# A new order for all five engines, small-tile work gathered, program blocks pinned, fixed PSUM banks and a fourth group slot in a four-layer cross-attention kernel

## The chip, the cores and the metric

The kernel runs on one core of one Trainium2 chip. The metric is the device time of that core in microseconds, the median of several executions; lower is better. TensorE (PE in the profile) multiplies, VectorE (DVE) and ScalarE (ACT) do elementwise work and empty PSUM, GpSimd (POOL) does elementwise work in SBUF, and SyncE (SP) issues DMAs.

## What is computed

Four cross-attention layers run one after the other on `x` (128 sequences of 64 tokens, 128 channels). Every layer attends to the same context `ctx_2048` (128 sequences of 64 tokens, 256 channels). All is float32. Layer 0 has 16 heads of 64 channels, a bias on a few key columns, and a dense output projection with bias:

```python
q = hidden_states @ Wq;  k = encoder @ Wk;  v = encoder @ Wv        # 16 heads of 64
logits = einsum('bhqd,bhkd->bhqk', q, k) * 64**-0.5 + col_bias      # 64 x 64 per head
out = einsum('bhqk,bhkd->bhqd', softmax(logits), v)
x = out @ Wo + bo + x
```

Layers 1 to 3 normalise `x` first (rmsnorm with a weight), have 16 query heads of 8 channels on 4 key and value heads, and add their output to `x`:

```python
q = (rmsnorm(x, norm_w) @ wq)      # (T, 4 kv heads, 4 repeats, 8)
k = cond @ wk;  v = cond @ wv      # (S, 4, 8)
attn = softmax(einsum('btgrd,bsgd->bgrts', q, k) / 8**0.5)
x = x + einsum('bgrts,bsgd->btgrd', attn, v) @ wo
```

## The kernel before, in words

The batch is cut into 32 groups (`NG`) of 4 sequences, 256 tokens a group; `x` and the context lie transposed, channels on partitions. A group's work is a set of steps, each named (kind, group, layer, part). A step's TensorE part, and what empties it, are:

- `k`, `v`, `k3`, `q0` (L935 to L969): projections of context and x for layer 0, and the small keys of layers 1 to 3 (`k3`); 128x128 weights, moving 256 to 374 columns. ScalarE copies them out.
- `s` of layer 0 (L980): scores, in 64x64 tiles of the array; VectorE adds the bias (`add`), takes the maximum (`max`), GpSimd subtracts (`sub`), ScalarE takes `exp`, VectorE `sum` and `rcp`, GpSimd normalises (`nrm`).
- `s` of layers 1 to 3 (L991): scores in 32x64 tiles; VectorE `max` and `sub`, ScalarE `exp` with the rmsnorm factor `inv` as its scale, VectorE `sum` and `rcp`, GpSimd `nrm`.
- `t` (L1009): transposes of the normalised scores, 64 rows by 128 columns each, with an identity as the moving operand; ScalarE copies them back (`et`).
- `pv0` (L1019, 64x64 tiles), `pv` of layers 1 to 3 (L1055, 128x32 tiles): probabilities times values. `wo0` (L1027) and `wo` (L1063): output projections in the full array, added to x by VectorE.
- `x2` (L1038): x transposed with full 128x128 identities, squared by ScalarE, summed by VectorE (`ssq`), turned into `inv` on GpSimd (`ms`). `q` (L1032): the query projection of layers 1 to 3.

Every fp32 matmul of the source is two matmul instructions in the trace, a transpose is one. Matmuls with fewer rows or columns than 128 use a part of the array, so that two to sixteen of them can run side by side.

SyncE loads x (`lt`) and context (`cT`) for three groups on, stores a group's result (`st`), and for layers 1 to 3 spreads the small keys into block-diagonal tiles (`kr`, 16 DMAs a layer and group, 48 a group, L858). All of it goes through one queue in a written order.

The order on each engine comes from tables of slots, one per engine (`PE_TIME`, `ACT_TIME`, and so on): a step of group g stands at g x `PERIOD` + its slot, and `timed` sorts the steps by that. Tables with the suffix `_ENDS` replace the slots of the groups at both ends (0 to 2 and 28 to 31). The slots set an order only; at run time each engine takes its list in order and waits on counting semaphores. A period of TensorE's list holds steps of four groups: projections of one, layer 0 of the next, layers 1 to 3 of older ones. The last two groups (`SPLIT`) are worked in halves of 128 tokens.

Three slots (`NS`) hold the per-group tiles `xT`, `QT`, `E`, `stat`, `inv`, `nt`; a group reuses those of the group three before it. The eight PSUM banks are given out while the program is written: a step takes the banks that, by the slot tables (`DUE`), come free first (`bank_of`), and waits for whoever emptied them last (`before`, `emptied`). An `s` step of layers 1 to 3 takes two adjacent pairs. A `t` step takes four banks, two for each half, and waits for each half by itself, inside one step.

Of the kernel before, what the change touches and what calls it, by code (L numbers as in the profile page):

```python
# [18 lines left out]
NS = 3  # L19
# [11 lines left out]

# [3 lines left out]

PERIOD = 42.042923
PE_TIME = {
    "k": {0: (-412.51237, -392.85979, -393.50182, -378.96658)},
    "v": {0: (-362.26897, -361.57101, -345.3867, -356.85139, -354.42587, -354.15549)},
    "k3": {0: (-370.81423,)},
    "q0": {0: (-376.11391, -371.17844, -371.03544, -374.58041)},
    "s": {0: (-370.42581, -370.43581), 1: (-331.1163,), 2: (-294.56971,), 3: (-270.23591,)},
    "t": {0: (-348.90236,), 1: (-317.45557,), 2: (-285.56016,), 3: (-253.49293,)},
    "pv0": {0: (-336.97107, -339.47402)},
    "wo0": {0: (-335.52959,)},  # L50
    "x2": {1: (-333.51029,), 2: (-300.02901,), 3: (-272.27314,)},
    "q": {1: (-333.36356,), 2: (-297.92571,), 3: (-272.42144,)},
    "pv": {1: (-307.00785,), 2: (-275.6979,), 3: (-251.97787,)},
    "wo": {1: (-306.84954,), 2: (-274.17148,), 3: (-249.78271,)},
}
ACT_TIME = {
    "k": {0: (-159.40091, -139.84623, -139.98107, -130.14834)},
    "v": {0: (-113.28983, -107.6489, -91.26426, -99.3201, -101.51439, -100.50468)},
    "k3": {0: (-118.80598,)},
    "q0": {0: (-126.45335, -120.46805, -119.7705, -121.20179)},  # L60
    "exp": {0: (-104.71249, -107.45298, -104.13778, -112.0564),
            1: (-72.87501, -75.24855, -75.86332, -77.67646),
            2: (-46.48173, -42.853, -38.45332, -45.85794),
            3: (-13.61974, -15.46628, -16.07173, -9.25001)},
    "et": {0: (-94.43216, -92.88175, -94.18051, -93.30054),
           1: (-65.47568, -65.49475, -67.04523, -58.9258),
           2: (-29.57269, -30.6792, -29.39678, -29.30645),
           3: (-5.91218, -5.28672, -5.87163, -4.79848)},
    "pv0": {0: (-88.61505, -90.21177)},
    "x2": {1: (-80.71806,), 2: (-48.9703,), 3: (-20.92127,)},  # L70
    "q": {1: (-83.14394,), 2: (-49.01262,), 3: (-21.83589,)},
    "pv": {1: (-54.62611,), 2: (-28.54234,), 3: (-2.96356,)},
}
DVE_TIME = {
    "add": {0: (-111.81915, -113.85763, -116.32868, -114.4835)},
    "max": {0: (-111.12099, -111.9694, -109.50874, -113.03448),
            1: (-78.27865, -78.64191, -80.16737, -81.16307),
            2: (-49.4951, -47.30671, -44.89232, -48.09597),
            3: (-18.00057, -19.96031, -20.47661, -12.65384)},
    "sum": {0: (-105.85858, -108.79654, -105.82451, -108.85157),  # L80
            1: (-74.06889, -72.89305, -74.39011, -76.6622),
            2: (-45.82444, -42.12155, -39.90611, -43.17731),
            3: (-11.25879, -13.61973, -15.19198, -8.91803)},
    "rcp": {0: (-105.30454, -105.8339, -104.88475, -105.95459),
            1: (-73.24416, -72.5981, -74.25837, -75.30566),
            2: (-43.71754, -41.14225, -36.69635, -42.40837),
            3: (-8.99609, -11.86286, -13.00823, -8.45231)},
    "wo0": {0: (-85.86089,)},
    "ssq": {1: (-83.37942,), 2: (-50.06193,), 3: (-24.55834,)},
    "sub": {1: (-75.05879, -76.58249, -77.57201, -79.06871),  # L90
            2: (-47.48804, -44.41007, -42.7565, -47.06613),
            3: (-15.77249, -17.39509, -18.78085, -11.73353)},
    "wo": {1: (-52.80331,), 2: (-24.91929,), 3: (0.43953,)},
}
POOL_TIME = {
    "sub": {0: (-109.0751, -112.84247, -103.46541, -114.27942)},
    "nrm": {0: (-96.88446, -97.18383, -96.68759, -99.16105),
            1: (-77.33025, -74.7097, -77.44776, -81.07111),
            2: (-47.81451, -39.53916, -39.48291, -39.86483),
            3: (-10.89236, -10.98157, -11.60033, -9.93748)},  # L100
    "ms": {1: (-90.05711,), 2: (-48.08021,), 3: (-16.64786,)},
}
SP_TIME = {
    "cT": {0: (-79.98433,)},
    "kr": {1: (-146.01496,), 2: (-158.22011,), 3: (-95.52327,)},
    "lt": {0: (-85.21396,)},
    "st": {0: (-22.10277,)},
# [15 lines left out]
    },
    1: {
        "k": {0: (-566.91726, -566.84726, -566.85909, -495.94114)},
        "v": {0: (-429.86277, -454.09358, -429.42785, -432.53711, -410.26388, -409.41835)},
        "k3": {0: (-451.20253,)},
        "q0": {0: (-443.81064, -543.11196, -443.80064, -566.90726)},
        "s": {0: (-435.74448, -435.73448), 1: (-361.36903,), 2: (-293.48868,), 3: (-270.59363,)},
        "t": {0: (-398.16561,), 1: (-327.25449,), 2: (-283.08701,), 3: (-254.95664,)},  # L130
        "pv0": {0: (-391.3161, -392.15936)},
        "wo0": {0: (-369.64937,)},
        "x2": {1: (-363.56604,), 2: (-294.08881,), 3: (-271.1829,)},
        "q": {1: (-365.31926,), 2: (-294.87445,), 3: (-272.68924,)},
        "pv": {1: (-319.44014,), 2: (-276.55088,), 3: (-252.35751,)},
        "wo": {1: (-303.22232,), 2: (-272.96424,), 3: (-250.92766,)},
    },
    2: {
        "k": {0: (-477.83204, -474.8597, -452.75348, -474.26973)},
        "v": {0: (-397.59961, -370.32494, -366.3626, -399.37273, -393.74967, -369.82342)},  # L140
        "k3": {0: (-436.78293,)},
        "q0": {0: (-438.05897, -412.93857, -411.14663, -405.14797)},
        "s": {0: (-401.02958, -370.42598), 1: (-332.3726,), 2: (-294.80438,), 3: (-270.32365,)},
        "t": {0: (-345.90875,), 1: (-316.53142,), 2: (-285.32115,), 3: (-252.84676,)},
        "pv0": {0: (-335.7855, -336.0694)},
        "wo0": {0: (-335.19552,)},
        "x2": {1: (-333.7359,), 2: (-307.00405,), 3: (-272.73062,)},
        "q": {1: (-332.77139,), 2: (-306.92719,), 3: (-272.48453,)},
        "pv": {1: (-312.76983,), 2: (-277.23482,), 3: (-251.66785,)},
        "wo": {1: (-310.567,), 2: (-275.19735,), 3: (-250.15637,)},  # L150
    },
    28: {
        "k": {0: (-412.71099, -395.62776, -394.66559, -374.46511)},
        "v": {0: (-372.72927, -370.61535, -348.22122, -356.11236, -372.30535, -369.1062)},
        "k3": {0: (-372.90485,)},
        "q0": {0: (-376.19535, -376.52669, -372.80769, -378.85152)},
        "s": {0: (-366.08291, -370.42578), 1: (-333.69106,), 2: (-294.56964,), 3: (-290.9334,)},
        "t": {0: (-348.95635,), 1: (-316.43043,), 2: (-291.45239,), 3: (-289.21552,)},
        "pv0": {0: (-337.34252, -348.14089)},
        "wo0": {0: (-335.38944,)},  # L160
        "x2": {1: (-335.13648,), 2: (-305.96072,), 3: (-291.1191,)},
        "q": {1: (-335.12648,), 2: (-295.55608,), 3: (-291.1291,)},
        "pv": {1: (-312.12718,), 2: (-291.32735,), 3: (-288.30154,)},
        "wo": {1: (-311.7751,), 2: (-291.19727,), 3: (-287.41173,)},
    },
    29: {
        "k": {0: (-416.8347, -394.81034, -399.13617, -389.50576)},
        "v": {0: (-375.72257, -375.58124, -353.93453, -354.84901, -372.30905, -368.8995)},
        "k3": {0: (-379.11161,)},
        "q0": {0: (-392.62609, -376.79767, -375.64799, -377.27179)},  # L170
# [432 lines left out]
        "st": {0: (-73.11023, -81.94464)},  # L603
    },
}
SPLIT = range(NG - 2, NG)
LATE = range(NG - 2, NG)


# [713 lines left out]
```

## Time and profile before

| | us |
|---|---|
| runs of the kernel before | 1378.57, 1382.42, 1383.25 |
| median | 1382.42 |
| span of the profiled execution | 1376.3 |
| own time of the profiled execution outside that span | not given by the page |
| TensorE busy in it | 1362.7 |
| VectorE, ScalarE, GpSimd busy | 1064.6, 1003.3, 734.9 |

The span runs from the first to the last instruction of the core; a run's time has what lies around it as well. A share of busy time is an average over the span. For matmuls the profile models the end, and those that run side by side overlap, so TensorE's share says that it always has something under way, not that it is at its peak; the distance from one step's start to the next one's is what a step takes. Line numbers are those of the kernel before.

### The profile page before, as it was taken

The page shows a single profiled execution, that of the slowest core. Times are in us where ns is not written, and L with a number is a line of the kernel's source. Part 1 is how long each engine was busy: PE and PEld are TensorE (multiplying, and loading weights), DVE is VectorE, ACT ScalarE, POOL GpSimd, SP SyncE. Part 2 cuts the span into 40 slices and gives each one's busy share as a digit, 9 for nine tenths or more (in the row PEclk, how much of TensorE's full clock was granted, in tenths as well). Part 3 has the DMA queues.
Part 4 walks back from the last instruction along what each step waited for, and adds up shares of the span by engine and source line. Part 5 has one row for each costly group of instructions (what it writes and reads, how often), then busy time and mean ns, then how long its engine had stood idle before and what let it go on. Part 6 is the DMA issues. An engine that isn't in the chain of part 4 may idle for free.

```text
span 1376.3 us, 59054 instructions
## 1 busy us (share of the span) xinstructions
PE 1362.7 (99%) x25494; PEld 1055.6 (77%) x25494; DVE 1064.6 (77%) x2258; ACT 1003.3 (73%) x2207; POOL 734.9 (53%) x851
## 2 busy tenths in 40 slices
PE   9999999999999999999999999999999999999997
PEld 7777777777777777777787777777777777777875
DVE  4487777987778977778777788777798777778776
ACT  4667777767778677777677786777776777767886
POOL 5355456654456545466554565544665445655553
PEclk9999999999999999999999999999999999999999
DMA  5010010000000010100001001001011010010000
GB/s 151 18 30 22 15 34 16 26 27 23 26 23 22 27 27 23 28 18 26 26 24 26 23 22 27 27 24 28 17 27 27 23 27 25 19 36 22 7 23 14
DMA packets 46003, 37.02 MB, mean 27 GB/s; under 512 B 17072, under 2 KB 41520, under 8 KB 45744
## 3 DMA queue, kind: packets, MB, share of 16 engines
q1 hardware_dynamic: 44576, 32.89, 8.8%
q8 instruction: 201, 3.29, 1.0%
q14 instruction: 58, 0.48, 0.1%
q10 hardware_dynamic: 1168, 0.36, 0.1%
HBM read 16.42 MB, written 4.19 MB: 15 GB/s over the span
## 4 chain that ended last, share of the span: by engine, by line
PE 95%; ACT 2%; DVE 2%; issue 0%; POOL 0%; DMA 0%; SPq 0%; POOLq 0%
PE psum L954 18%; PE psum L942 16%; PE psum L1009 10%; PE psum L1027 8%; PE psum L969 8%; PE psum L991 7%; PE psum L1055 7%; PE psum L1019 5%; PE psum L980 5%; PE psum L1063 4%; PE psum L1032 3%; PE psum L961 2%; PE psum L1038 2%; ACT E L1141 1%; ACT E L1136 1%; DVE st L1226 1%
## 5 line engine op out<-in xcount | busy, mean ns | idle before, releaser
L892 POOL TENSOR_TENSOR E<-E,st 128x512 f32<-128x512 f32 x488 | 497.3, 1044 | 168.1 <-DVE st L1238 159.4
L1136 ACT ACTIVATE E<-E,inv 128x512 f32<-128x512 f32 x384 | 273.4, 722 | 135.8 <-DVE E L1230 134.3
L1226 DVE TENSOR_REDUCE st<-psum 128x8 f32<-128x512 f32 x372 | 240.4, 673 | 145.5 <-PE psum L991 145.1
L1235 DVE TENSOR_REDUCE st<-E 128x8 f32<-128x512 f32 x488 | 321.2, 665 | 35.3 <-ACT E L1129 28.2
L1141 ACT COPY E<-psum 128x512 f32<-128x512 f32 x512 | 275.1, 609 | 33.7 <-PE psum L1009 33.5
L954 PE MATMUL psum<-wv,cT 128*128 128x374 f32 (+1 forms) x768 | 273.3, 486 | 0.3 <-issue 0.3
L1230 DVE TENSOR_TENSOR E<-psum,st 128x512 f32<-128x512 f32 x372 | 248.3, 677 | 0.3
L904 POOL TENSOR_TENSOR nt<-nt,powers 128x2 f32<-128x2 f32 (+1 forms) x102 | 19.9, 196 | 420.0 <-DVE nt L1265 400.2
L942 PE MATMUL psum<-cT,wk 128*128 128x256 f32 x1024 | 240.5, 383 | 0.2 <-DMA cT<-in_ctx_t 0.2
L942 PEld LDWEIGHTS psum<-cT,wk 128*128 128x128 f32 x1024 | 191.5, 190 | 34.8 <-issue 1.5
L954 PEld LDWEIGHTS psum<-wv,cT 128*128 128x128 f32 x768 | 138.2, 189 | 73.5 <-ACT V L1097 8.5
L888 POOL TENSOR_TENSOR E<-E,st 128x512 f32<-128x512 f32 x140 | 142.6, 1044 | 35.8 <-DVE st L1220 13.1
L1009 PE MATMUL psum<-ident,E 64*128 64x64 f32 x4096 | 156.6, 226 | 3.5 <-issue 1.4
L1009 PEld LDWEIGHTS psum<-ident,E 64*128 64x128 f32 x4096 | 138.3, 139 | 20.0 <-issue 8.0
L969 PE MATMUL psum<-xq,wq 128*128 128x256 f32 x512 | 129.0, 385 | 0.0
L1027 PE MATMUL psum<-QT,wo 128*128 128x256 f32 (+1 forms) x544 | 119.1, 372 | 0.5 <-ACT QT L1163 0.5
L1055 PEld LDWEIGHTS psum<-E,VB 128*32 128x32 f32 x6144 | 90.9, 110 | 37.1 <-issue 14.7
L1097 ACT COPY V<-psum 128x374 f32<-128x374 f32 (+1 forms) x192 | 87.3, 456 | 42.9 <-PE psum L954 42.1
L1121 ACT ACTIVATE QT<-psum 128x512 f32<-128x512 f32 x128 | 75.9, 599 | 56.5 <-PE psum L969 48.2
L969 PEld LDWEIGHTS psum<-xq,wq 128*128 128x128 f32 x512 | 94.8, 190 | 23.1 <-issue 10.8
L991 PE MATMUL psum<-KB,QT 32*64 32x256 f32 x3072 | 109.2, 388 | 1.6 <-ACT QT L1160 1.0
L1027 PEld LDWEIGHTS psum<-QT,wo 128*128 128x128 f32 x544 | 96.2, 190 | 14.8 <-ACT QT L1163 0.6
(68 smaller groups left out, 1632.2 us busy)
## 6 DMA issues: line engine op xcount, KB each, us to landing
KB<-K SPq DMA_DIRECT2D x1536, 8.0 KB
cT<-in_ctx_t SPq DMA_DIRECT2D x32, 256.0 KB, 2.8
xq<-in_x_t SPq DMA_DIRECT2D x32, 128.0 KB, 2.1
out<-xT SPq DMA_DIRECT2D x30, 128.0 KB, 1.8
wk<-in_L_xattn_Wk SPq DMA_DIRECT2D x3, 256.0 KB, 5.8
wv<-in_L_xattn_Wv SPq DMA_DIRECT2D x2, 374.0 KB, 8.6
wq<-in_L_xattn_Wq SPq DMA_DIRECT2D x1, 512.0 KB, 7.7
wo<-in_L_xattn_Wo SPq DMA_DIRECT2D x1, 512.0 KB, 4.4
```

The source lines that it names most:

```text
L892: e.tensor_tensor(E3, E3, wide(stat[s][u][:, 16:24]), ALU.mult).then_inc(g_nrm.sem, 1)
L942: m = e.matmul(bank[:, T * jj:T * jj + T], wk0[:, k, 128 * j:128 * j + 128], cTg[:, k, :], start=(k == 0), stop=(k == 1))
L954: m = e.matmul(bank[:, 0:hi - lo], cTg[:, k, 128 * p:128 * p + 128], wv[:, k, lo:hi], start=(k == 0), stop=(k == 1))
L969: m = e.matmul(bank[:, T * jj:T * jj + T], wq0[:, 128 * j:128 * j + 128], xq[g % NX][:, :], start=True, stop=True)
L991: m = e.matmul(psum[64 * b2:64 * b2 + 64, at[r], 256 * p:256 * p + 256], QT[s][lo:lo + 32, 0, 64 * b:64 * b + 64], KB[l - 1][g % 2][lo:lo ...
L1009: m = e.transpose(psum[:, at[2 * n + i], c:c + 64], E[s][2 * p + r][rows, 128 * k:128 * k + 128], ident[rows, rows])
L1027: m = e.matmul(bank[:, tokens], wo0[:, j, :], QT[s][:, j, tokens], start=(j == 0), stop=(j == 7))
L1136: e.activation(E[s][u][:, :], E[s][u][:, :], ACT.Exp, scale=inv[s][:, u // 2:u // 2 + 1]).then_inc(a_exp.sem, 1)
L1141: e.copy(E[s][u][:, :], psum[:, i, :]).then_inc(a_et.sem, 1)
L1226: e.tensor_reduce(stat[s][u][:, 0:8].rearrange("p (r h) -> p r h", r=2), scores_of[g, l, u], AX, ALU.max).then_inc(d_max.sem, 1)
L1230: e.tensor_tensor(pairs(E[s][u][:, :]), scores_of[g, l, u], stat[s][u][:, 0:8].rearrange("p (r h a) -> p r h a", r=2, a=1).to_broadcast([1 ...
L1235: e.tensor_reduce(stat[s][u][:, 8:16], heads(E[s][u][:, :]), AX, ALU.add).then_inc(d_sum.sem, 1)
```

## The change

1. All slot tables are new. `PERIOD` is 41.111607 instead of 42.042923 (both only scale the ordering). Groups 0 to 6 and 26 to 31 have tables of their own, and those replace a group's slots altogether. The new order gathers the steps that use small tiles. From one `wo0` to the next TensorE's list was (kind and layer; brackets around small-tile steps; letters without a layer are layer 0 or projections):

```
before: wo0 q0 wo3 x2.1 q1 q0 [s1] q0 q0 k3 k [s0 s0 t2] v v [pv2 t1] wo2 v q3 x2.3 v [s3] v k k [pv1 t0] wo1 v
        x2.2 q2 [pv0 t3 pv0] k [s2 pv3]
after:  wo0 q0 q1 q0 [s1 x2.1 t3.1] k q0 v v k3 [t3.0 t2.1 s0 s0 t1.1 t1.0 t2.0] k k [pv3 pv2 pv1] wo3 wo2 q0 q3
        [x2.3 t0.0 t0.1 s3] v k wo1 v v q2 [pv0 s2 x2.2 pv0] v
```

Over all groups the list changes between full-array and small-tile steps 470 times before and 384 times after.

2. A `t` step is one half of a group (`t` part 0 and part 1), with its own slot, two banks and its own waits; it was both halves in one step.
3. `x2` is done as transposes of 64 rows, the same tile shape as `t`: four instead of two per group and layer, into two adjacent banks. ScalarE's square reads both banks with a strided pattern.
4. Before the steps in `FRESH` (part 1 of `t` in layers 0 and 3; other sets at the ends) the TensorE program is aligned to a multiple of 256 instructions. The loader branches over the padding.
5. The banks of each step stand in tables (`PE_BANKS`, `BANK_ENDS`); `DUE` and the search are gone.
6. `NS` is 4 instead of 3.

```diff
-NS = 3
+NS = 4
...
-PERIOD = 42.042923
+PERIOD = 41.111607
 PE_TIME = {
...
-    "t": {0: (-348.90236,), 1: (-317.45557,), 2: (-285.56016,), 3: (-253.49293,)},
+    "t": {0: (50.12134, 50.61734), 1: (81.13632, 80.58731), 2: (122.74371, 119.08386), 3: (159.64587, 152.83728)},
...
+FRESH = {("t", 0, 1), ("t", 3, 1)}
+FRESH_ENDS = {
+    0: {("t", 0, 1), ("t", 3, 1)},
+    1: {("t", 3, 1)},
+    2: {("t", 3, 1)},
+    3: {("t", 0, 1), ("t", 3, 1)},
+    4: {("t", 0, 1), ("t", 3, 1)},
+    5: {("t", 0, 1), ("t", 3, 1)},
+    6: {("t", 0, 1), ("t", 3, 1)},
+    26: set(),
+    27: {("pv0", 0, 1), ("q0", 0, 2), ("v", 0, 4), ("wo", 3, 0), ("x2", 3, 0)},
+    28: set(),
+    29: {("t", 1, 0)},
+    30: {("pv0", 0, 0), ("v", 0, 3), ("x2", 3, 1)},
+    31: set(),
+}
...
-        for kind, layers in {**table, **{k: {**table.get(k, {}), **v} for k, v in at_ends.get(g, {}).items()}}.items():
+        for kind, layers in at_ends.get(g, table).items():
...
-DUE = {tuple(st): at for at, *st in ACT_TIMED + DVE_TIMED}
+
+
+def banks_of(kind, g, l, u):
+
+    return [int(i) for i in BANK_ENDS.get(g, PE_BANKS)[kind][l][u]]
...
-            return [[st]] * (2 if kind == "pv0" else 1)
+            return [[st]] * (2 if kind in ("pv0", "x2") else 1)
...
-            evictors = held_until(st)
-            if st[0] == "s" and l > 0:
-                at = min(([i, i + 1, j, j + 1] for i in range(5) for j in range(i + 2, 7)),
-                         key=lambda four: max(free[i] for i in four))
-            else:
-                at = sorted(sorted(range(8), key=lambda i: free[i])[:len(evictors)])
+            evictors, at = held_until(st), banks_of(*st)
+            assert len(at) == len(set(at)) == len(evictors)
...
-                if kind != "t":
-                    emptied(w, [ev for evs in before[st] for ev in evs])
+                emptied(w, [ev for evs in before[st] for ev in evs])
+                if (kind, l, u) in FRESH_ENDS.get(g, FRESH):
+                    e.addr_align(256, max_nops=0)
...
                     for p in halves(g, u):
-                        m = e.transpose(bank[:, 128 * p:128 * p + 128], xT[s][:, 128 * p:128 * p + 128], ident[:, :])
+                        for i in range(2):
+                            rows = slice(64 * i, 64 * i + 64)
+                            m = e.transpose(psum[:, at[i], 64 * p:64 * p + 64], xT[s][rows, 128 * p:128 * p + 128],
+                                            ident[rows, rows])
...
+                    p = halves(g, u)
+                    x = psum[:, at[0]:at[0] + 2, 64 * p[0]:64 * p[-1] + 64].rearrange("t i (p c) -> t i p c", c=64)
+                    sq = QT[s][:, 2, tokens].rearrange("t (p i c) -> t i p c", i=2, c=64)
...
-                        e.activation(QT[s][:, 2, tokens], bank[:, tokens], ACT.Square).then_inc(a_ev.sem, 1)
+                        e.activation(sq, x, ACT.Square).then_inc(a_ev.sem, 1)
```

## Rows read from the trace of the kernel before

**Rows 1.** The page, part 1: busy us, share of the span, instructions.

```profile
PE 1362.7 (99%) x25494; PEld 1055.6 (77%) x25494; DVE 1064.6 (77%) x2258; ACT 1003.3 (73%) x2207; POOL 734.9 (53%) x851
```

**Rows 2.** The page, part 4: shares of the chain by engine.

```profile
PE 95%; ACT 2%; DVE 2%; issue 0%; POOL 0%; DMA 0%; SPq 0%; POOLq 0%
```

**Rows 3.** Windows: stretch, its length, busy us of each engine (instructions), clock.

```profile
160.00:1120.00 960.00, 957.42 (x17869) 742.01 (x17868) 763.64 (x1626) 713.56 (x1559) 526.86 (x598) 1.00 0.09 24
...
1330.00:1376.00 46.00, 38.23 (x1084) 28.41 (x1082) 32.89 (x62) 31.51 (x74) 16.01 (x26) 1.00 0.06 17
```

**Rows 4.** TensorE timeline, steady: start, us, line, tile, count.

```profile
681.67 1.42 PE L954 MATMUL psum<-wv,cT 128*128 128x374 f32 x4
682.93 0.59 PE L1032 MATMUL psum<-xT,wqs 128*128 128x256 f32 x2
...
683.58 1.42 PE L954 MATMUL psum<-wv,cT 128*128 128x374 f32 x4
684.93 1.12 PE L991 MATMUL psum<-KB,QT 32*64 32x256 f32 x32
685.98 1.52 PE L954 MATMUL psum<-wv,cT 128*128 128x372 f32 x4
687.33 3.62 PE L942 MATMUL psum<-cT,wk 128*128 128x256 f32 x16
...
694.84 0.38 PE L1038 MATMUL psum<-ident,xT 128*128 128x128 f32 x2
695.05 0.60 PE L1032 MATMUL psum<-xT,wqs 128*128 128x256 f32 x2
...
696.67 1.21 PE L1009 MATMUL psum<-ident,E 64*128 64x64 f32 x32
697.82 1.16 PE L1019 MATMUL psum<-E,V 64*64 64x64 f32 x64
...
701.88 1.10 PE L1055 MATMUL psum<-E,VB 128*32 128x64 f32 x64
702.91 3.72 PE L1027 MATMUL psum<-QT,wo 128*128 128x256 f32 x16
```

**Rows 5.** TensorE timeline near the end: t in a half, pv in four runs.

```profile
1340.36 0.71 PE L1009 MATMUL psum<-ident,E 64*128 64x64 f32 x16 [0.22 <-ACT E L1136]
1341.00 0.49 PE L1063 MATMUL psum<-QT,wos 128*128 128x128 f32 x2
...
1357.97 0.65 PE L1049 MATMUL psum<-E,ones 128*32 128x64 f32 x32
...
1359.89 1.07 PE L1063 MATMUL psum<-QT,wos 128*128 128x128 f32 x4
```

**Rows 6.** Timeline: first wo0 matmuls of groups 3, 17 and 26.

```profile
156.08 1.78 PE L1027 MATMUL psum<-QT,wo 128*128 128x256 f32 x7
...
744.76 1.56 PE L1027 MATMUL psum<-QT,wo 128*128 128x256 f32 x6
...
1123.28 1.99 PE L1027 MATMUL psum<-QT,wo 128*128 128x256 f32 x8
```

**Rows 7.** Timeline: a t step stopped in its middle.

```profile
632.05 0.90 PE L1009 MATMUL psum<-ident,E 64*128 64x64 f32 x22
633.94 0.53 PE L1009 MATMUL psum<-ident,E 64*128 64x64 f32 x10 [0.99 <-issue]
```

**Rows 8.** The page, part 3: the queue that brings instructions.

```profile
q8 instruction: 201, 3.29, 1.0%
```

**Rows 9.** SyncE timeline: copies of the small keys.

```profile
672.09 10.99 SPq L858 DMA_DIRECT2D KB<-K  x16
...
683.62 21.67 SPq L858 DMA_DIRECT2D KB<-K  x32
```

**Rows 10.** Timeline: group 0, s1 and its t.

```profile
44.40 1.12 PE L991 MATMUL psum<-KB,QT 32*64 32x256 f32 x32
...
65.43 1.21 PE L1009 MATMUL psum<-ident,E 64*128 64x64 f32 x32
```

More of the change, by code:

```diff
@@ L65 @@
[L65 to L72, printed above, removed]
+    "k": {0: (2.50397, 14.44440, 4.26196, -8.93698)},
@@ L73 @@
+    "pv0": {0: (62.41330, 60.00031)},
+    "x2": {1: (70.81265,), 2: (102.44397,), 3: (132.58655,)},
+    "q": {1: (68.69162,), 2: (100.48978,), 3: (132.33356,)},
+    "pv": {1: (88.79163,), 2: (129.00702,), 3: (169.71564,)},
 }
 DVE_TIME = {
[L75 to L79, printed above, removed]
@@ L88 @@
[L88 to L93, printed above, removed]
+    "add": {0: (38.62964, 39.22464, 39.81964, 40.41464)},
+    "max": {0: (41.60565, 42.20166, 41.00964, 42.79767),
+            1: (72.65164, 73.84564, 71.13165, 70.53564),
+            2: (103.35898, 102.76297, 104.87897, 102.16696),
+            3: (136.96619, 135.17413, 137.56219, 134.57812)},
@@ L138 @@
-    2: {
[L139 to L150, printed above, removed]
+        "k": {0: (29.85090, 26.29356, 28.12423, 32.41656)},
@@ L173 @@
[L173 to L178 removed]
+        "k": {0: (-11.60978, -11.61170, -11.61362, -63.42667)},
+        "v": {0: (52.38427, 61.31826, 42.08233, -11.60956, 46.31366, 3.65048)},
@@ L481 @@
+        "sum": {0: (63.13143, 61.71542, 52.88674, 57.06078)},
+        "rcp": {0: (64.54147, 64.43246, 58.85079, 62.90743)},
+        "wo0": {0: (76.73003, 73.08739)},
+        "sub": {1: (89.49072, None, 87.58172, None),
[5 rows of a table added]
     },
     31: {
[L483 to L487 removed]
@@ L502 @@
+        "wo0": {0: (55.97612, 60.60253)},
+        "sub": {1: (65.93248, None, 70.23485, None),
[5 rows of a table added]
     },
@@ L603 @@
-        "st": {0: (-73.11023, -81.94464)},
-    },
+        "cT": {0: (12.16878,)},
+        "kr": {1: (38.07344,), 2: (49.82106,), 3: (72.22179,)},
+        "lt": {0: (83.27184,)},
+        "st": {0: (107.63390, 108.70116)},
+    },
+}
+PE_BANKS = {
+    "k": {0: ("6", "7", "0", "6")},
+    "v": {0: ("5", "4", "2", "7", "0", "5")},
+    "k3": {0: ("1",)},
+    "q0": {0: ("6", "6", "7", "4")},
+    "s": {0: ("17", "63"), 1: ("0123",), 2: ("1245",), 3: ("0123",)},
+    "t": {0: ("54", "67"), 1: ("01", "42"), 2: ("57", "25"), 3: ("40", "47")},
+    "pv0": {0: ("03", "30")},
+    "wo0": {0: ("0",)},
+    "x2": {1: ("56",), 2: ("67",), 3: ("01",)},
+    "q": {1: ("7",), 2: ("1",), 3: ("7",)},
+    "pv": {1: ("3",), 2: ("2",), 3: ("5",)},
+    "wo": {1: ("6",), 2: ("2",), 3: ("4",)},
+}
@@ L759, in xattn_kernel @@
             for i, evs in zip(at, evictors):
-                held[i], free[i] = evs, max(DUE[ev] for ev in evs)
+                held[i] = evs
             if st[0] == "s" and l == 0:
```

1395 lines of the change are left out of this document (977 added, 418 removed), and 102 rows, old and new, of tables (BANK_ENDS, DVE_ENDS, PE_ENDS).

## The prediction

> **What bounds the kernel now.** I read the busy shares first, then the windows, then the chain, then TensorE's order of work in time. TensorE is busy 1362.7 us of a span of 1376.3 [rows 1]; VectorE has 77%, ScalarE 73%. The chain that ended last is TensorE for 95% [rows 2]. Between 160 and 1120 us TensorE is busy 957.42 of 960 us at full granted clock, while VectorE has 763.64, ScalarE 713.56 and GpSimd 526.86; only in the last 46 us does TensorE idle much, 46.00 - 38.23 = 7.8 us [rows 3]. So nothing that waits elsewhere is worth anything between the ends. What is left is the time that TensorE spends on what it does, and that depends on order: in the steady stretch each step has a fixed time set by its neighbours, to 0.01 us [rows 4]. The reader is to look there at start-to-start times, not at the second column, in which a matmul's end is modelled and overlaps the next.
>
> **Price of a change of tile shape.** The same v step of 4 matmuls takes 681.67 to 682.93 = 1.26 us between full-array steps, 683.58 to 684.93 = 1.35 before a 32x64-tile step, and 685.98 to 687.33 = 1.35 behind one (372 columns there, so 1.25 undisturbed) [rows 4]. A full-array run between small-tile steps thus pays 0.09 + 0.10 = 0.19, which I round to 0.20. The small side pays too. A t step with 32 transposes takes 697.82 - 696.67 = 1.15 us, one with 16 takes 1341.00 - 1340.36 = 0.64 [rows 4, 5]; 16 more cost 0.51, so the run itself holds 0.64 - 0.51 = 0.13, say 0.14 (other t rows give 1.14). Sixty-four pv matmuls take 702.91 - 701.88 = 1.03; 128 in one run, four rows of x32, take 1359.89 - 1357.97 = 1.92; the second 64 cost 0.89, and a run holds 0.14 [rows 4, 5]. A row of neighbours of the same shape pays each price once.
>
> The Trainium skill says why, in TensorEngine Tiling (Array Packing), Key Properties: a change of tiling mode drains the engine, a change of tile within a mode does not. It gives no price. The trace has one, but it shows more than the sentence: a small-to-small change costs as well.
>
> **The change, part by part.**
> (1) The order of TensorE. I counted runs of one shape over the two lists of steps, from one wo0 to the next. Before: full 7, s 3, 64x64 tiles (s0 and pv0) 3, t 4, pv 3. After, in five small stretches of the steady period (six is the mean with the ends, 384 / 2 / 32): full 5, s 3, 64x64 3, t with x2 5, pv 1. The difference is 2 x 0.20 full + 2 x 0.14 pv - 1 x 0.14 t = 0.54 us a group.
> (2) x2 becomes four 64-row transposes into two banks. Now it is 0.21 us in a full run [rows 4], three times a group; at t's rate, 0.51 / 16 = 0.032 each, four cost 0.13. Gain 3 x 0.085 = 0.26. The runs that it breaks are in (1). The bounds are 0.63 (x2 vanishes beside its neighbours) and -0.16 (each x2 pays 0.14 more than I counted). I take 0.26, from the t rows, whose tile shape and operands it has.
> Together 0.80 us a group. Undisturbed, a period takes 744.76 - 702.91 = 41.85 us [rows 4, 6]; it becomes 41.05. There are 23 such periods, 156.08 to 1123.28, so 18.4 us. At the ends the groups have orders of their own. Over all, full/small changes drop from 470 to 384, that is 43 stretches fewer, of which the 23 periods give 46; same-shape runs drop from 659 to 620, 39 fewer against 69 in the steady part (20 to 17 a period). So the ends have 30 runs more, at 0.14 some 4.3 us, less 9 groups x 0.26 = 2.3 for x2: 2.0. Work: -18.4 + 2.0 = -16.4.
> (3) Alignment. The mean of the 23 periods is 967.20 / 23 = 42.05, 0.20 more than an undisturbed one, 4.6 us in all [rows 6]. The rows of a stall show what it is: a t step stops in its middle for 0.99 us with no one to blame but "issue" [rows 7]. The instruction queue brought 201 packets of 3.29 MB / 201 = 16.4 KB [rows 8]; TensorE has 2 x 25494 = 50988 loads and matmuls, 254 a packet. So the program comes in blocks of 256 instructions, 128 matmuls, and a block that is used up in 2 us outruns the next one. The five stalls of the steady part all stand in small-tile runs, this one behind 128 s0 matmuls. After, the dense places are denser: three pv in a row are 192 matmuls in 3 x 0.89 + 0.14 = 2.8 us. The two alignments pin where blocks begin: from t0.1 to t3.1 are 302 matmuls, 2.4 blocks, from there to the next t0.1 486, 3.8. Walking the order with the times above, the shortest block (rest of s0, three t, a little k) lasts 3.8 us, the one that holds most of the pv run 4.7. I take all 4.6 us as gone (bounds 0, and +1 us a group, below). By a page's rule it would be otherwise: the Trainium skill, Runtime: NRT & Kernel Launch, Instruction fetch mechanics, holds the crossing of a block boundary for mostly hidden. Then nothing is gained here and the time is that of rival E; rows 7 speak against it.
> What alignment adds is a jump over the padding, 59 in all (38 in groups 7 to 25, 12 before, 9 after) and one block more to fetch in most groups. No row shows a jump on TensorE. From below it is 0: the target block was asked for a whole block ago, and instructions already queued cover it. From above it is a full stall, 0.99 us each [rows 7]. I take 0, the nearest case being the clean boundaries, six a group, that leave periods at 41.85.
> (4) Four slots. From q0 to the last wo a group now stays in flight for 4.0 periods; slots only keep that legal. SP's queue: the 48 KB copies a group take 10.99 + 21.67 = 32.7 us of the period [rows 9]; with the loads and the store 34.1 of 41.05. From k3 to s1 of the same group TensorE has 34 us of other steps, and two sets of copies and their landing need about 24, so 10 us cover this. An added wait there would hold the x load and the context load queued behind it, each needed two periods later.
> (5) Banks. Fixed ones change no duration. x2 now needs two; VectorE's and ScalarE's part is unchanged, and their shares become 763.64 / 957.42 x 41.85 / 41.05 = 81% and 76%, nowhere a bound. What is queued behind a t that waits for its bank is all of TensorE, so an error there costs in full (second rival).
> (6) The ends. In flight for a period more, the first group runs with less beside it. Before, s1 of group 0 starts at 44.40 and its t at 65.43, 21 us later [rows 10]; in the new order only eight steps, x2, q0, k, two v, k3 and two s0, about 9 us, stand between, and VectorE alone needs four units of max, sub, sum and reciprocal, 4 x 1.9 = 7.6, plus an exp and a normalisation of 1.0, 9.5 to 10. That is a wait of about 1 us, and I count six such places in groups 0 to 2. At the far end the last 46 us hold 7.8 us of idle already [rows 3], and the new list interleaves groups 28 to 31 more finely. Bounds 0 and 12 us more idle; I take 8, as much again as the end has now.
>
> **Sum.** -16.4 - 4.6 + 8 = -13.0 us on a span of 1376.3, so 1363.3. The profiled span lies 6.1 under the median of the runs, 1382.42 (runs 1378.57 to 1383.25); the page gives no other time of its own execution. I keep the 6.1: 1369.4 us, 0.9% faster.
>
> **Rivals.**
> (A) No extra idle at the ends, gain in full: 1369.4 - 8 = 1361. For it, the start of before loses only little; against, the short chain of (6). 0.10.
> (B) TensorE waits once a group, on a bank or a normalisation, because steps of one shape now stand together and their evictions come in bursts: ten copies of transposes of 0.5 us each around one stretch, with 3.5 us of k before the pv. A wait of 0.5 us in 23 groups gives back 11.5: 1381. For it, bursts; against, 19 to 24% spare time on both engines and nothing in rows 3 that waits. 0.13, half of it ending below 1378.
> (C) A jump over padding stalls TensorE. Each costs up to 0.99 us [rows 7]; the change turns slower from 13.0 / 59 = 0.22 us a jump; at 0.5 us it is +29.5, 1399. For it, jumps stand inside small-tile stretches, where the queue is drained fastest; against, clean boundaries cost nothing. 0.08. The Trainium skill, Runtime: NRT & Kernel Launch, Instruction fetch mechanics, speaks of a stall when a taken branch leaves the two pages held; the target here is the next page, so by it this rival is out.
> (D) The dense runs outrun the fetch in spite of the alignment, because a block of 3.8 us is still too short: about 1 us a group, +23, 1392. 0.05. One block of 2 us stalled in before, one of 3.8 did not show, so the threshold lies between.
> (E) The small stalls stay as they are, 0.20 us a period, because jumps and the more frequent fetches give back what pinned boundaries save: 1369.4 + 4.6 = 1374. For it, one fetch more in most groups; against, the densest blocks are the ones pinned away. 0.08.
>
> **Chances and range.** The forecast has 0.56, with 1363 to 1374 as its own range (extra idle 2 to 12). What a measurement of this kernel tells from no change is about 0.3%, 4.1 us. Faster: 0.56 + 0.10 + 0.08 and half of B, 0.06, = 0.80; same: the rest of B and 0.01 of mild C = 0.08; slower: C and D, 0.12. The range goes from 1360 to 1386: it leaves out the strong forms of C and D.
>
> **What would show it.** wo0 to wo0 at 41.0 to 41.1 us in nearly every steady period, with no long "issue" gap; one pv run of x192 of about 2.8 us; x2 at 0.13 beside t; the v steps beside small tiles still at 1.35. A period of 41.3 to 41.6 with releasers named is B; gaps before t0.1 and t3.1 are C; gaps in the middle of pv or s0 are D. TensorE idle in the first 130 and the last 60 us should be about 18 us, where it is 10 now. If undisturbed periods come out at 41.85, the price of a shape change was misread and the prediction is wrong at its root.

## The result, and the profile after

| | before | after |
|---|---|---|
| time, median of the runs | 1381.6 us (1378.57 to 1383.25) | 1430.9 us (1420.92 to 1433.51) |
| profiled execution: time, span | -, 1376.3 us | 1430.16, 1428.4 us |

The ratio is 1.034, 95% interval 1.031 to 1.038. I had predicted 1369.4 us, 0.9% faster; it became 3.4% slower, outside the range.

The page after, part 1, then the instruction queue of part 3 and the chain's shares of part 4:

```profile
PE 1370.1 (96%) x25686; PEld 1058.6 (74%) x25686; DVE 1081.4 (76%) x2258; ACT 1018.0 (71%) x2207; POOL 734.2 (51%) x851
...
q8 instruction: 223, 3.65, 1.1%
...
PE 80%; DVE 10%; POOL 5%; issue 2%; ACT 2%; DVEq 0%; POOLq 0%
```

TensorE was 99% busy [rows 1] and is 96%: 58 us of the span idle where there were 14. It works only 7 us longer. There are 22 block fetches more [rows 8]. TensorE's share of the chain fell from 95% [rows 2] to 80%, as it seems because the chain runs through releasers that are falsely named for the long waits below; in d2, a run below that has none of these waits, it is 93%. The windows say where, and the list of TensorE's waits of after (total us, times, longest) says at which tile:

```profile
160.00:1120.00 960.00, 924.61 (x17340) 718.53 (x17339) 750.11 (x1564) 695.22 (x1501) 503.71 (x572) 0.99 0.09 24
1382.40:1428.40 46.00, 37.84 (x1170) 28.90 (x1154) 34.00 (x67) 33.48 (x73) 17.98 (x28) 1.00 0.06 18
```

```profile
PE psum L1602 <- POOL E L1486: 29.8, 19, 2.7
PE psum L1602 <- issue: 6.2, 23, 0.7
```

The steady stretch idles 35.4 us (2.6 before, [rows 3]), the last 46 us little more than before (8.2 against 7.8). L1602 is the t step. The view names GpSimd's normalisation as the releaser of 19 waits. Four of them, 1.6 us, stand in the first 110 us. The other 15, 28.2 us, stand in the steady stretch; there the normalisation had been done, as the runs below show, and "issue" would be the right word. A long wait ahead of t3.1, one with the half clock behind it, and the same place without a stall (timeline of after):

```profile
611.58 0.34 PE L1633 MATMUL psum<-ident,xT 64*128 64x64 f32 x4
614.13 0.71 PE L1602 MATMUL psum<-ident,E 64*128 64x64 f32 x16 [2.21 <-POOL E L1486]
...
655.69 0.34 PE L1633 MATMUL psum<-ident,xT 64*128 64x64 f32 x4
658.09 1.12 PE L1602 MATMUL psum<-ident,E 64*128 64x64 f32 x16 [2.05 <-POOL E L1486]
659.13 3.08 PE L1537 MATMUL psum<-cT,wk 128*128 128x256 f32 x8
662.05 1.03 PE L1564 MATMUL psum<-xq,wq 128*128 128x256 f32 x4
...
701.14 0.34 PE L1633 MATMUL psum<-ident,xT 64*128 64x64 f32 x4
701.31 0.66 PE L1602 MATMUL psum<-ident,E 64*128 64x64 f32 x16
701.95 1.99 PE L1537 MATMUL psum<-cT,wk 128*128 128x256 f32 x8
703.78 1.03 PE L1564 MATMUL psum<-xq,wq 128*128 128x256 f32 x4
```

x2 to t takes 2.55, 2.40 and 0.17 us. The record of the jump itself, the branch over the padding (L1523), tells the first of these places from the last: it took 2782 ns where the t came late and 297 ns where it did not (views of L1523 around either):

```profile
L1523 PEldq COMPARE_BRANCH  x1: 2782/2782/2782, 611.3 to 611.3; - x1
...
L1523 PEldq COMPARE_BRANCH  x1: 297/297/297, 700.9 to 700.9; - x1
```

Of the 23 jumps ahead of t3.1 in groups 3 to 25, 16 stall so: x2 to t takes 1.0 to 3.1 us, 0.8 to 2.9 over the 0.17. Behind 658.09 the same eight k matmuls take 662.05 - 659.13 = 2.92 us instead of 1.83, and the t ahead of them 1.04 instead of 0.64: the granted clock was 0.5 for 3.4 us, as at three other places, each behind one of these stalls (x2 to t 2.0 to 2.4 us). Behind the five longest stalls, 2.55 to 3.07 us, it stayed at 1.0. The other jump, between t0.0 and t0.1, has its gap in every group, and the dense run of pv is as predicted, 719.55 - 716.73 = 2.82 us, with no stall in it:

```profile
694.25 2.11 PE L1620 MATMUL psum<-QT,wo 128*128 128x256 f32 x9
...
716.73 2.89 PE L1651 MATMUL psum<-E,VB 128*32 128x64 f32 x192
719.55 1.13 PE L1659 MATMUL psum<-QT,wos 128*128 128x256 f32 x4
...
722.08 0.66 PE L1602 MATMUL psum<-ident,E 64*128 64x64 f32 x16
722.99 0.71 PE L1602 MATMUL psum<-ident,E 64*128 64x64 f32 x16 [0.26 <-issue]
...
736.14 2.12 PE L1620 MATMUL psum<-QT,wo 128*128 128x256 f32 x9
```

t to t takes 0.91 us here and 0.5 without a jump; over the whole period the jump costs 0.47 (41.89 here, 41.42 in d1 below, whose other steps are the same). And the period without a long stall, 736.14 - 694.25 = 41.89 us, is no shorter than before (41.85, [rows 4, 6]).

### The profile page after: what moved, and what is told of

It reads as the page before. It is cut to its first block, busy times and chain, and to the rows that moved or that the text cites. A ratio compares the mean times of both kernels' runs of the same rounds, so it can differ in the third digit from the quotient of the medians.

```text
span 1428.4 us, 59381 instructions
## 1 busy us (share of the span) xinstructions
PE 1370.1 (96%) x25686; PEld 1058.6 (74%) x25686; DVE 1081.4 (76%) x2258; ACT 1018.0 (71%) x2207; POOL 734.2 (51%) x851
## 4 chain that ended last, share of the span: by engine, by line
PE 80%; DVE 10%; POOL 5%; issue 2%; ACT 2%; DVEq 0%; POOLq 0%
PE psum L1537 16%; PE psum L1549 15%; PE psum L1602 10%; PE psum L1586 6%; PE psum L1651 6%; PE psum L1564 5%; POOL E L1486 5%; PE psum L1575 4%; PE psum L1620 4%; PE psum L1612 4%; PE psum L1659 3%; DVE E L1828 3%; DVE st L1824 3%; PE psum L1625 3%; DVE st L1833 2%
## 5 line engine op out<-in xcount | busy, mean ns | idle before, releaser
L1737 ACT COPY E<-psum 128x512 f32<-128x512 f32 x512 | 266.6, 599 | 76.3 <-PE psum L1602 73.2
L1732 ACT ACTIVATE E<-E,inv 128x512 f32<-128x512 f32 x384 | 260.2, 720 | 40.1 <-POOL inv L1500 29.3
L1537 PE MATMUL psum<-cT,wk 128*128 128x256 f32 x1024 | 249.8, 392 | 1.0 <-ACT KT L1685 0.7
L1828 DVE TENSOR_TENSOR E<-psum,st 128x512 f32<-128x512 f32 x372 | 243.8, 683 | 0.4
L1602 PE MATMUL psum<-ident,E 64*128 64x64 f32 x4096 | 163.3, 226 | 41.2 <-POOL E L1486 29.8
L1602 PEld LDWEIGHTS psum<-ident,E 64*128 64x128 f32 x4096 | 141.9, 139 | 69.5 <-POOL E L1486 32.3
L1685 ACT COPY KT<-psum 128x512 f32<-128x512 f32 x128 | 75.8, 592 | 49.6 <-PE psum L1537 48.9
L1811 DVE TENSOR_TENSOR E<-psum,bias 128x512 f32<-128x512 f32 x128 | 80.4, 684 | 24.2 <-PE psum L1575 24.1
```

Source lines behind the costliest of these rows:

```text
L1537: m = e.matmul(bank[:, T * jj:T * jj + T], wk0[:, k, 128 * j:128 * j + 128], cTg[:, k, :], start=(k == 0), stop=(k == 1))
L1602: m = e.transpose(psum[:, at[i], c:c + 64], E[s][2 * u + r][rows, 128 * k:128 * k + 128], ident[rows, rows])
L1732: e.activation(E[s][u][:, :], E[s][u][:, :], ACT.Exp, scale=inv[s][:, u // 2:u // 2 + 1]).then_inc(a_exp.sem, 1)
L1737: e.copy(E[s][u][:, :], psum[:, i, :]).then_inc(a_et.sem, 1)
L1828: e.tensor_tensor(pairs(E[s][u][:, :]), scores_of[g, l, u], stat[s][u][:, 0:8].rearrange("p (r h a) -> p r h a", r=2, a=1).to_broadcast([1 ...
```

## The experiments

"Mean period" is from group 3's wo0 to group 25's, in 22 parts: 42.03 us before, 43.67 after.

**a1, a2, a3, b1: where the stalls come from.** a1 is after with all alignments taken out; a2 lacks only those at t3.1, a3 only those at t0.1; b1 is before with two added.

```
a1  -  if (kind, l, u) in FRESH_ENDS.get(g, FRESH): e.addr_align(256, max_nops=0)
a2  +  if (kind, l, u) in FRESH_ENDS.get(g, FRESH) - {("t", 3, 1)}: ...
a3  +  if (kind, l, u) in FRESH_ENDS.get(g, FRESH) - {("t", 0, 1)}: ...
b1  +  if 2 < g < 26 and (kind, l, u) in {("t", 0, 0), ("t", 3, 0)}: e.addr_align(256, max_nops=0)
```

> The changed kernel without any alignment of the program; all else as changed. Theory J (the jumps over padding stall TensorE, because the block jumped to is fetched late): the gaps of up to 2.5 us before part 1 of t in layer 3 and of 0.3 us before part 1 of t in layer 0 go; undisturbed periods come to 41.0 to 41.4 us, small stalls stay where a block is used up inside pv or s0; time 1365 to 1385. Rival O (the new order itself waits, on GpSimd's normalisation as the profile names it): the gaps stay, time 1420 to 1440. Rival F (without pinned blocks the dense pv run outruns the fetch in many groups): gaps of about 1 us in pv or s0 in most groups, time 1390 to 1410.

> The changed kernel with the alignment before part 1 of t in layer 3 taken out and all others kept. Theory J: the 2 us gaps go, the 0.3 us ones at layer 0 stay, plus a random stall where block ends fall badly: 1375 to 1395. Rival O: 1420 to 1440.

> The changed kernel with only the alignment before part 1 of t in layer 0 taken out. If the 2 us gap depends on the block that is jumped from being left early (50 matmuls in), its size changes with the new place of the block ends: a group has now 1.6 thousand instructions between two jumps and leaves its last block after about 60 instructions. Theory J: still some gap before part 1 of t in layer 3, 0 to 3 us a group, time 1380 to 1440. Rival O: 1420 to 1440 with gaps as they were.

> The kernel before, order and banks untouched, with the same alignment before t of layer 0 and t of layer 3 in groups 3 to 25. Theory J: each of the 46 jumps costs 0.3 to 2.5 us by where it leaves its block, so 1395 to 1450 against 1382, with gaps only before these t steps. Rival O: the alignment is harmless, 1375 to 1385.

Measured: a1 1417.8 us (ratio 1.027, 1.025 to 1.029), a2 1506.8 (1.091, 1.088 to 1.095), a3 1463.7 (1.062, 1.056 to 1.068), b1 1434.4 (1.038, 1.036 to 1.041); mean periods 42.76, 46.88, 45.26 and 44.25. Only b1 fell where I had expected it. a1 came out between the ranges of its theories, and a2 and a3 above all of theirs, so the first form of the theory was too mild: one badly placed jump a group costs more than two. In b1 nothing but two jumps a group came into the old order, and it has after's stall and its false releaser (waits of b1):

```profile
PE psum L1011 <- POOL E L892: 35.5, 20, 3.2
```

So the alignment is guilty: b1 has the order and the normalisation of before. But without alignment the new order is slow as well. Its waits in a1 (L1649 pv, L1600 t, L1573 s0):

```profile
PE psum L1649 <- issue: 13.2, 12, 1.6
PE psum L1600 <- issue: 5.0, 10, 1.1
PE psum L1573 <- issue: 4.2, 5, 1.2
```

That is rival D's mechanism: dense runs outrun the fetch. All but one of its "issue" gaps in the steady stretch end 2.3 to 3.0 us after a fetch began. a2 and a3 show what makes a jump dear. I walked the order with its undisturbed times: in a2 52 instructions stand in the last block ahead of the jump, used up in 1.8 us, and another block lasts 2.1 us; in a3 the last one is used up in 1.1 us. The block behind the jump seems to be asked for only when the last block is entered, and from the fetch's start to the next matmul the traces show 2.3 to 3.1 us, median 2.5 (116 stalled jumps of after, a2, a3, b1, c1, c2, e1 and f2).

**c1, c2, f2: where the boundaries fall.** Only the slots of the two alignments differ from after (here a slot is the place in a block of 256 at which the aligned step begins).

```
c1  e.addr_align(256, offset=16 if l == 0 else 0, max_nops=0)
c2  e.addr_align(256, offset=16 if l == 0 else 32, max_nops=0)
f2  e.addr_align(256, offset=8 if l == 0 else 0, max_nops=0)
```

> The kernel after, with t0.1 aligned to slot 16 of a block instead of slot 0, so that every block boundary up to t3.1 comes 16 instructions earlier; the last of them then lies inside wo0 and no longer just ahead of q's wait for wo0's eviction. Theory J (a jump is free only if the block behind it was asked for some 3 us or more before, and TensorE's sequencer cannot ask while it stands at a wait close behind the boundary): the stalls ahead of t3.1, 0.9 to 3.0 us in 16 of 22 periods, vanish in all of them, the half-clock stretches of 3.4 us that followed them too, the 0.475 us a group at t0.1 stay. Mean period 43.67 -> 41.9 to 42.0, time 1430 - 38 = 1392 (1386 to 1400). Rival P (each jump over padding has a price of its own, whatever block it leaves): nothing changes by more than 0.1 us a group, 1428 to 1432. Rival O (the t3.1 steps wait for GpSimd's normalisation): the same 1428 to 1432.

> As c1, and t3.1 aligned to slot 32, so that the boundaries behind it come 32 instructions earlier. In the walk through the undisturbed times of the order, one block then holds s0, three t and no k and is used up in 2.6 us (in c1 the shortest takes 3.8). Theory J, with blocks coming at least some 3.5 us apart: a stall of about 0.9 us inside s0 or t in nearly every group, mean period 42.8, time c1 + 20 = 1412 (1402 to 1420), although the number of jumps and fetches is that of c1. Rival P: as c1 within 3 us.

> The kernel after with t0.1 at slot 8, t3.1 at slot 0: the last boundary lies 20 instructions ahead of q's wait (12 in after: 16 of 22 groups stalled; 27 in c1: none). Theory H: stalls of 1 to 3 us ahead of t3.1 in some 5 to 12 of 22 groups, mean period 42.4 to 43.2, time 1408 to 1427. Rival L (it is the length of the last block that decides, 103 instructions here, 95 in after, 111 in c1, with a sharp limit): every group the same, either 1402 or 1430, and the fetch ahead of the jump always starts at the same distance from the boundary.

Measured: c1 1401.8 us (1.014, 1.012 to 1.016), c2 1413.2 (1.022, 1.020 to 1.024), f2 1429.1 (1.037, 1.033 to 1.041). Sixteen slots took 29 us away. In c1 none of the t3.1 jumps stalls and nearly every period is 41.9, though nothing of the normalisation was changed; the waits at t keep only the small gap of t0.1:

```profile
PE psum L1602 <- issue: 5.7, 23, 0.3
```

c1's time was 10 us over my figure: the mean period, 42.08, was only 0.1 over; 8.0 us lie behind group 25, and most of them at one place. There the jump ahead of an aligned x2 stalls in c1 (a branch of 3.93 us) and not in after (0.39), and a half-clock stretch of 6.8 us follows it. The steps from the q in front of it to the second q0 behind take 16.07 us instead of 10.22. The x2 in c1:

```profile
1262.67 0.48 PE L1633 MATMUL psum<-ident,xT 64*128 64x64 f32 x4 [3.35 <-issue]
```

The same jump stalls in e1, f1 and f2 (2.8 to 3.4 us), so the times of these runs hold it as well; mean periods do not. c2 lost 0.55 us a group to its 2.6 us block, where I had said 0.9. f2 corrects the theory: with 20 instructions between the boundary and q's wait 17 of 23 jumps stall, about as with 12, and I had expected 5 to 12 of them. The start of the last fetch relative to the jump has two values in after and f2: 5.2 to 7.3 us ahead (no stall), or between 1.4 us ahead and 0.8 behind; in c1 only the first. The wait itself dates them. q waits for wo0's addition to x, and passes 4.3 us after wo0 begins. In groups 3 to 24 of after, f2, c1 and of e1 and f1 below, the last fetch starts 2.5 to 4.6 us ahead of that moment in all 67 jumps without a stall, and 0.9 to 3.1 us behind it in all 43 with one, never between. So the request is held by the wait or it is not. With 23 instructions (e1) 10 of 22 jumps stall, with 27 (c1) and 31 (f1) none, so the limit lies between 23 and 27 instructions. Why the same code comes out one way in one group and the other way in the next is open. The Trainium skill, Runtime: NRT & Kernel Launch, Instruction fetch mechanics, says that the sequencer fetches the next page while it executes the current one. The traces agree, with one fetch for every 256 instructions [rows 8] and the early fetches above, and add that the fetch can be held back by a wait in the current one.

**c3, d3, d1, c4: the price of a jump itself.** One alignment a group, in full-array steps with long blocks around it.

```
c3  after emptied(...):   if 2 < g < 26 and (kind, l, u) == ("v", 0, 4): e.addr_align(256, offset=64, max_nops=0)
d3  the same lines, ahead of emptied(...)
d1  if 2 < g < 27 and (kind, l, u) == ("q0", 0, 3): e.addr_align(256, offset=160, max_nops=0)
c4  before.py: if 3 < g < 27 and (kind, l, u) == ("q0", 0, 0): e.addr_align(256, offset=32, max_nops=0)
```

> The kernel after with one alignment a group (3 to 25) instead of two, at v4, a full-array step, to slot 64. In the walk no block of the group is used up in less than 4.0 us, and the block left by the jump lasts 5.8 us. Theory J: the jump costs about 0.1 us, the stalls inside pv, t and s0 go. Mean period 41.5 (41.40 undisturbed, 42.76 without alignment, 43.67 with the two); time 1417.8 - 28 = 1390 (1385 to 1396), the rest over the kernel before being its ends. Rival F (the dense run of 192 pv matmuls outruns the fetch wherever blocks begin): stalls of 1 to 1.8 us in pv stay in many groups, 1405 to 1418. Rival P: 0.5 us or more for each of 23 jumps, 1400 or more.

> The kernel before with one alignment a group (4 to 26), at the first q0 behind wo0, to slot 32. In the walk no block is used up in less than 3.8 us. Theory J: the 4.6 us of small fetch stalls go, 23 jumps at 0.1 us come: 1380.3 - 4.6 + 2.3 = 1378 (1375 to 1381), period 41.95 in every group. Rival P: 23 x 0.5 = 11 us or more on top, 1388 or more (two alignments at t0.0 and t3.0 gave 1434).

> The kernel with one alignment a group at v4 and slot 64, with the alignment put ahead of v4's wait for its bank instead of behind it; nothing else differs. In that kernel the trace has the wait, then a branch of 0.30 to 0.38 us, then the matmul, and v to v takes 0.88 us instead of 0.38. Theory J2: the branch is now done while the four matmuls of v1, 1.25 us, run, and the wait comes behind it: v to v 0.38 to 0.45, mean period 41.93 -> 41.45, 1390 (1386 to 1394). Rival P2: 0.88 us stay, 1398 to 1402.

> The kernel after with one alignment a group (3 to 26), ahead of the q0 that follows wo0, to slot 160. Theory J2 (a jump costs TensorE 0.3 to 0.45 us from the branch to the next matmul, paid in full where the branch stands behind a wait that is met just in time, and nothing where its sequencer gets to it while matmuls are still queued): here 16 matmuls of wo0, 3.4 us, are queued, so the jump is free, and no block is used up in less than 3.7 us. Mean period 41.45 (41.93 with the jump at v4), time 1400.3 - 22 x 0.48 = 1389.7 (1386 to 1394). Rival P2 (a jump costs about 0.5 us in this order wherever it stands): 1398 to 1402, a gap ahead of q0.

Measured: c3 1400.3 us (1.012, 1.011 to 1.014), d3 1389.8 (1.007, 1.005 to 1.009), d1 1388.7 (1.006, 1.004 to 1.008), c4 1382.2 (1.000, 0.999 to 1.001). c3 missed its 1390 although its blocks are long: every v4 comes late (timeline, then waits of c3),

```profile
555.55 0.48 PE L1549 MATMUL psum<-wv,cT 128*128 128x374 f32 x1
556.44 1.52 PE L1549 MATMUL psum<-wv,cT 128*128 128x374 f32 x4 [0.41 <-issue]
```

```profile
PE psum L1549 <- issue: 9.5, 24, 0.4
```

and the trace has the reason between the two: the wait for the bank, passed at 555.92, a branch of 0.30 us at 556.09, the matmul at 556.44. With the branch one line up, ahead of the wait, v to v is 0.38 and the whole program 10.5 us faster. In d1 and c4 the branch is reached while wo0's matmuls are queued and costs nothing: the undisturbed periods of c4 are 41.85, those of d1 41.42. In c4 the block even comes late, the branch lasts 0.38 to 3.49 us with a median of 2.89, and wo0's 3.5 us cover it. The t3.1 jump of c1 is free too, x2 to t 0.17. A jump thus costs 0.4 to 0.5 us behind a wait that is met just in time (0.91 - 0.50 at t0.1, 0.89 - 0.38 at v4), nothing under queued work, and 1 to 4 us where the block was asked for late and nothing covers it (4.0 at most, in a2).

c4 missed its 1378 (1375 to 1381). The small fetch stalls that it was to remove are still there: pv0 stops 8 times in the steady stretch, 3.2 us in all and up to 1.1, though the walk had no block under 3.8 us, and the mean period is 42.11 against 42.03. So pinning gave the old order nothing, and a walk with no short block does not rule a stall out; what delays those fetches was not looked into.

**d2: the alignments of the last groups.** d1 plus those of groups 27, 29 and 30 as after has them.

> As d1, and the alignments of groups 27, 29 and 30 as the kernel after has them. The part behind group 25's wo0 took 299 us in after and 305 to 308 without any alignment there, with stalls in pv and pv0. Theory J2: the alignments at the end are worth about 4 us, 1385 (1382 to 1390). Rival (they are worth nothing, the difference is in disturbed clock): as d1 within 2 us.

Measured 1385.6 us (1.0034, 1.0023 to 1.0045), 3.1 under d1. It is the best form of the new order, and still 0.3% slower than before.

**e1, f1, f3: what the new x2 is worth.** x2 as full transposes again, on c1, on c1 with slot 24, and on d2.

```
-  for i in range(2): rows = slice(64 * i, 64 * i + 64)
-      m = e.transpose(psum[:, at[i], 64 * p:64 * p + 64], xT[s][rows, 128 * p:128 * p + 128], ident[rows, rows])
+  m = e.transpose(bank[:, 128 * p:128 * p + 128], xT[s][:, 128 * p:128 * p + 128], ident[:, :])
```

> The kernel c1 (alignments at slots 16 and 0, undisturbed periods 41.90) with x2 as one 128x128 transpose per half again, into one bank, as in the kernel before. The prediction's prices: x2 0.21 instead of 0.13 us, three times; between s and t one more full-array run, 0.20; between s and pv0 a full-array run 0.20 in place of a small one 0.14. Sum 0.25 + 0.20 + 0.06 = 0.51 us a group: mean period 42.08 -> 42.6, undisturbed 41.90 -> 42.41, time 1401.8 + 0.51 x 29 = 1417 (1412 to 1420). Rival S (a change of shape costs nothing, only x2's own time counts): +0.25 a group, 1409.

> As e1 (x2 as full 128x128 transposes, two alignments a group), with t0.1 at slot 24 instead of 16, so that the last boundary ahead of q's wait lies 27 instructions before it instead of 19. Theory H (the request for the next block is held by an unmet wait that stands within about 20 instructions behind the boundary): the 10 stalls of 22 go, mean period 43.16 -> 42.1, time 1402 to 1405, as c1 with the new x2 (1401.8), since what the new x2 saves, 0.32 us a group by the start-to-start times, comes back as waits. Rival P3 (the form of x2 brought the stalls, by its shape): 1425 or more. Rival W (nothing is given back): 1401.8 + 0.32 x 29 = 1411.

> The kernel d2 (one alignment a group ahead of the q0 behind wo0, and those of the last groups) with x2 as full 128x128 transposes again. In d2 the undisturbed period of 41.42 holds about 0.3 us of waits. If the new x2's saving is given back as waits: mean period 41.61 -> 41.65 to 41.75, time 1386 to 1389 (d2 1385.6). If it is real: +0.32 x 29 = 9 us, 1395.

Measured: e1 1437.8 us (1.039, 1.034 to 1.045), f1 1401.4 (1.015, 1.014 to 1.017), f3 1391.7 (1.008, 1.007 to 1.010). e1 is a miss on time, because four instructions fewer between t0.1 and q's wait moved the boundary from 27 to 23 ahead of the wait (not to 19, as f1's expectation has it) and the stall came back in 10 groups:

```profile
604.12 0.44 PE L1631 MATMUL psum<-ident,xT 128*128 128x128 f32 x2
606.25 0.71 PE L1602 MATMUL psum<-ident,E 64*128 64x64 f32 x16 [1.69 <-POOL E L1486]
```

f1 moves it to 31 and the stalls are gone. Its undisturbed period is 41.93, c1's 41.91: there the new x2 is worth nothing, though step by step it saves 0.20 between s and t, 0.02 between q and t0.1 and 0.10 between s and pv0, 0.32 together. What it saves comes back at once: two v steps take 2.69 us in c1 and 2.51 in e1, their matmuls starting 0.38 and 0.42 us after one another, instead of 0.31. The first of these two waits for a bank that VectorE's subtraction (L1828) frees 0.04 us before. In d2 and f3 these two v steps take the same 2.69 and 2.51. In f3 the loss is real but small, 0.13 us a group and 6.1 us in all; I had expected 1386 to 1389.

## Why the prediction was wrong

Of the 52.1 us by which the profiled span grew, 9.7 lie ahead of group 3's wo0 (165.8 instead of 156.1), 36.2 between there and group 25's, 6.2 behind. The 36.2 are about 31.5 of t3.1 stalls (those up to group 25's wo0), 22 x 0.47 = 10.4 at t0.1, 6.3 of half clock (t3.1 to the q0 behind it takes 4.0 to 4.1 us four times, 2.47 otherwise) and 22 x 0.19 = 4.2 in a few periods at either end of the stretch that are longer in every version of this order, less 22 x 0.43 = 9.5 for the shorter undisturbed period and 3.9 of small stalls that before had; that makes 39. Some 2 of the 3 us over come back in the stalled periods themselves, each 0.1 to 0.2 us shorter than 41.89 with its stall and half clock added.

- **Part (3) is the step that failed.** "The target block was asked for a whole block ago, and instructions already queued cover it", hence 0 for 59 jumps. The block is asked for some instructions after the last one is entered, and often late if a wait stands close behind its first instruction; and queued instructions cover the jump only where no wait stands before it. I had walked the lengths of the full blocks and not of the last, partial one, nor looked at what waits behind a boundary. The bound of 0.99 us a jump, from a boundary crossed in sequence [rows 7], was no bound: stalls reached 2.9 us in after and 4.0 in a2. Rival C had the mechanism with a chance of 0.08, on the argument that clean boundaries cost nothing; a boundary crossed in full stride says little of one reached by a jump. Against it I also had the Trainium skill, Runtime: NRT & Kernel Launch, Instruction fetch mechanics, which speaks of a stall where a taken branch leaves the two pages held. The runs show one for the very next block as well, while that is not yet loaded.
- **"I take all 4.6 us as gone"** compared the new order with before, not with itself: without alignment its denser runs lose 1.2 us a group (mean period 42.76 in a1, 41.61 in d1). The five stalls of before were also not all of one kind: four stand in small-tile runs, one of 0.3 us in a v step. What a short block does was right: no stall in pv in the steady stretch of after, stalls in c2 and a2 where the walk has 2.6 and 2.1 us. Pinning is worth having in the new order, at the right places (d1, d3); it was worth nothing in the old one (c4).
- **Parts (1) and (2), 0.80 us a group, are mis-sized: 0.43** (41.85 to 41.42 in d1). The step times are as priced (pv x192 2.82, v steps 1.35), but I sized the sum as if nothing waited. x2 measures 0.32 step to step against 0.51 by my prices, and 0.13 or 0.02 net; with the old x2 the order alone gives 41.85 - 41.56 = 0.29 instead of 0.54. Of the gap 0.18 is named by e1 as waiting of the two v steps; the rest I did not take apart. This is rival B in small. The sign that I had set for a misread price, undisturbed periods at 41.85, seems to have come, 41.89 in after; but 0.47 of that is the jump at t0.1, so the price of a change of shape was too high (0.54 for the order, 0.29 measured) and not misread at its root.
- **Part (6), the ends.** TensorE's idle in the first 130 us went from 2.2 to 8.8 us, as sized; group 3's wo0 is 9.7 us late, so 3 us are work or order. The last 46 us idle 8.2 us against 7.8, yet 6 to 8 us are lost behind group 25 in after and d2, with fetch stalls in a1 (pv and pv0 there) and 3 us of them removed by d2's alignments. Ends +16 where I had +10. That the first groups wait on the short chain of four slots is read from the code; no run tested it, though after and c1 both have four waits for GpSimd's normalisation there, 1.6 us in all.
- **Parts (4) and (5)** held in the main: the lists of waits name none for a group slot. But fixed banks did cost something: the 0.18 us above begin with a v step whose bank VectorE frees just too late. Neither the fourth slot nor the bank tables were varied by themselves.

So d2 stands 22 x 0.42 = 9 us better than before in the middle, 8 worse at the start and 7 to 8 at the end, which is its +0.3%. The gain of the change is real and smaller than what its ends cost, and the alignments as placed cost 45 us on top (after against d2). No version here beats the kernel before; what would is this order's middle with the old ends, which needs a plan for the passage between them and was not tried.

## What to carry to other kernels

When a program is aligned or jumps, walk its blocks with the trace's times, the last partial one too: ask how long it lasts, what wait stands within some 25 instructions behind its beginning, and put the jump under queued full-array work and ahead of the wait, not behind it. A few instructions more or fewer anywhere upstream move all of this (four in e1: 36 us), so a comparison of two small edits in such a kernel needs the boundaries held still. And a saving on a saturated engine is the change of its period, not the sum of its steps.

## What the runs showed of the hardware

- From the start of an instruction fetch to the matmul that needed it: 2.3 to 3.1 us, median 2.5, over 116 stalled jumps; fetches start at least 3.0 us apart in after, 3.4 in before.
- A jump over padding: a branch of 0.28 to 0.40 us on TensorE in after where the block is there, and of 1.2 to 3.3 us ahead of a stalled t3.1.
- A request for the next block can be held by an unmet wait 12, 20 or 23 instructions behind the boundary (16 of 23, 17 of 23 and 10 of 22 jumps); with 27 and 31 it never was. Held, it started 0.9 to 3.1 us after the wait was met.
- A late block costs nothing under queued work: in c4 the branch lasts 2.89 us at the median, under 16 matmuls of 3.5 us.
- Behind four of the 16 stalls in after the granted clock fell to 0.5 (1.2 instead of 2.4 GHz) for 3.4 us; it cost 1.6 us each. Behind the five longest it did not fall.
- The releaser that a profile names for a stalled instruction can be one that was done before: 15 of the 16 stalls bear the name of a GpSimd line. The length of the branch's own record tells them apart.
